# GpSimd issues the old rows of a batch, then the new rows of the batch before it

## The reference, cut to what matters

```python
x = x + einsum('bct,bcd->bdt', x, w0[cond])              # layer 0
q, k, v = x @ Wq.T, x @ Wk.T, x @ Wv.T                   # layer 1: 8 query heads, 4 key heads of 64
q, k = rope(rms(q)), rope(rms(k))
k_blocks = k_blocks.at[blk, :, off, :].set(k)            # all batches write their new rows first
v_blocks = v_blocks.at[blk, :, off, :].set(v)
k_all, v_all = k_blocks[block_tables], v_blocks[block_tables]
scores = q . k_all * SCALE, masked to the last 256 positions
x = x + softmax(scores) . v_all @ Wo.T
x = x + x @ W2[id] + b2[id]                              # layer 2: a 512x512 matrix per batch
x = x + x @ W3.T + adapter(x)                            # layer 3
```

## Time and profile before

| | |
|---|---|
| three runs | 1181.35, 1186.06, 1185.53 us (median 1185.53) |
| profiled execution | 1187.99 us, of which its span 1186.2 us |
| mean granted TensorE clock | 0.955 of full |
| PE busy | 1058.9 us (89% of the span) |
| DVE, ACT busy | 653.4 us (55%), 539.3 us (45%) |
| POOL busy | 532.8 us (45%) |
| gathers of old rows, L971 | 192, 999 ns each; POOL idle ahead of them 132.8 us |
| gathers of new rows, L981 | 192, 990 ns each; POOL idle ahead of them 281.7 us |

### The profile page before, as it was taken

The page is one execution under the profiler, slowest core; times in us unless marked ns, Lnnn a source line. Parts: engine busy times, 40 slices in busy tenths (PEclk is TensorE's granted clock), DMA queues, the critical chain, the costliest instruction groups (busy, mean ns, idle before and its releaser), DMA issues.

```text
span 1186.2 us, 23800 instructions
## 1 busy us (share of the span) xinstructions
PE 1058.9 (89%) x6440; PEld 709.0 (60%) x6440; DVE 653.4 (55%) x1888; ACT 539.3 (45%) x1336; POOL 532.8 (45%) x597
## 2 busy tenths in 40 slices
PE   4999999999159799999999999999999999999997
PEld 2767777877135556556556656556656556656555
DVE  5889785377234455555555555545555545455542
ACT  3457765475134344434444434444444444444440
POOL 1545444245545545544545444545544544444400
PEclk9999998899657899999999999999999999999998
DMA  3334443353263566655666655666655666655640
GB/s 123 115 134 142 136 138 110 109 175 134 82 203 98 159 203 211 191 178 172 196 193 205 203 180 172 195 192 212 198 180 172 193 192 206 203 181 173 196 143 18
DMA packets 95336, 196.15 MB, mean 165 GB/s; under 512 B 31346, under 2 KB 40114, under 8 KB 87110
## 3 DMA queue, kind: packets, MB, share of 16 engines
q1 hardware_dynamic: 63942, 149.49, 37.5%
q0 software_dynamic: 30784, 44.16, 14.2%
q10 hardware_dynamic: 576, 2.10, 0.5%
HBM read 195.08 MB, written 33.56 MB: 193 GB/s over the span
## 4 chain that ended last, share of the span: by engine, by line
PE 55%; DVE 5%; issue 3%; ACT 3%; DMA 1%; ACTq 0%; DVEq 0%
PE bank L90 18%; PE bank L1292 10%; PE bank L1246 8%; PE bank L1267 8%; PE bank L1233 4%; PE bank L1254 4%; DVE SM L1130 3%; ACT PT L1052 2%; PE bank L1223 2%; ACT KT L1052 1%; DVE XAL L1124 1%; DVE XAM L1173 1%; DMA KV<-kv_scratch,idxs 1%; DVE XAH L1178 1%; DVE nb L1134 0%
## 5 line engine op out<-in xcount | busy, mean ns | idle before, releaser
L981 POOL DMA_INDIRECT KV<-kv_scratch,idxs x192 | 190.1, 990 | 281.7 <-DMA KV<-in_pool,idxs 242.7
L1130 DVE CUSTOM_DVE_ANT_0 SM<-bank,FM 128x336 f32<-128x336 f32 x256 | 129.8, 507 | 249.7 <-PE bank L1246 228.7
L971 POOL DMA_INDIRECT KV<-in_pool,idxs x192 | 191.8, 999 | 132.8 <-issue 75.8
L1052 ACT ACTIVATE PT<-bank 112x384 f32<-112x384 f32 x256 | 111.7, 487 | 291.8 <-PE bank L1254 291.0
L1061 ACT ACTIVATE PR<-SM,nb 128x336 f32<-128x336 f32 x256 | 146.0, 577 | 1.0 <-DVE nb L1134 0.8
L1267 PE MATMUL bank<-PT,KV 112*64 112x128 f32 x1536 | 114.0, 285 | 27.4 <-ACT PT L1052 27.4
L1267 PEld LDWEIGHTS bank<-PT,KV 112*64 112x64 f32 x1536 | 86.6, 139 | 77.1 <-issue 40.0
L1052 ACT ACTIVATE KT<-bank 128x336 f32<-128x336 f32 x128 | 57.7, 451 | 159.7 <-PE bank L1233 159.1
L1292 PE MATMUL bank<-W,XT 128*64 128x512 f32 x512 | 123.7, 604 | 0.7 <-ACT XT L1052 0.7
L1246 PE MATMUL bank<-KT,QB 64*128 64x336 f32 x512 | 112.0, 515 | 5.6 <-ACT KT L1052 5.1
L90 PE MATMUL bank<-wqh,XTH 128*128 128x512 f32 x256 | 108.3, 423 | 9.2 <-DVE XTL L480 8.7
(11 more groups left out here) (157 smaller groups left out, 1931.5 us busy)
## 6 DMA issues: line engine op xcount, KB each, us to landing
W<-in_w SPq DMA_DIRECT2D x64, 1024.0 KB, 8.4
FM<-mask SPq DMA_DIRECT2D x64, 168.0 KB, 4.1
X<-in_x SPq DMA_DIRECT2D x32, 256.0 KB, 2.9
x_scratch<-X SPq DMA_DIRECT2D x32, 256.0 KB, 2.1
kv_scratch<-KVR SPq DMA_DIRECT2D x32, 256.0 KB, 2.4
qt_scratch<-QT SPq DMA_DIRECT2D x32, 256.0 KB, 2.9
QB<-qt_scratch SPq DMA_DIRECT2D x32, 256.0 KB, 2.8
XB<-x_scratch SPq DMA_DIRECT2D x32, 256.0 KB
```

Of the source, the lines that this page charges most:

```text
L971: pool.indirect_dma_start(out=KV[k][:, c, :], out_offset=None, in_=t["pool"], in_offset=bass.IndirectOffsetOnAxis(ap=idxs[k][:, c:c + 1], ...
L981: pool.indirect_dma_start(out=KV[k][:, c, :], out_offset=None, in_=kv_d, in_offset=bass.IndirectOffsetOnAxis(ap=idxs[k][:, NCH + c:NCH + c ...
L1052: return nc.scalar.activation(dst, src, ACT.Copy)
L1130: v.tensor_tensor_reduce(out=SM[u % 2][:, :], in0=bank[u % 2][:, 0:SPAN], in1=FM[k][:, :], scale=1.0, scalar=-3e38, op0=ALU.add, op1=ALU.m ...
```

## The change

In `body` on GpSimd the two helpers are called in another order, and `fresh` is moved out of `body` and takes the pair as an argument. Each batch's new rows are now issued one step later, behind the old rows of the batch that follows it. The last batch's new rows are issued behind the loop.

```diff
-                    def fresh(b):
-                        k = 2 * pr.par + b
...
-                    for b in range(2):
-                        held(b)
-                        fresh(b)
+                    held(0)
+                    if not (isinstance(p, int) and p == 0):
+                        fresh(pr.move(-1), 1)
+                    held(1)
+                    fresh(pr, 0)
+
+                def fresh(pr, b):
+                    k = 2 * pr.par + b
+
+                    wait_all(pool, s_pass_pool, (s_old[k], at(pr.i, 16 * NCH, 16 * NCH - 1)))
+                    for c in range(NCH):
+                        pool.indirect_dma_start(
...
                 bodies(pool, body)
+                fresh(Pair(PAIRS // 2 - 1, 1), 1)
```

More of the change, by code:

```diff
@@ L974, in held @@
                                 bounds_check=NPOOL * BLOCK - 1, oob_is_err=False).then_inc(s_old[k], 16)
-                    def fresh(b):
-                        k = 2 * pr.par + b
[L979 to L984, removed]
-                    for b in range(2):
-                        held(b)
-                        fresh(b)
+                    held(0)
[8 more added lines that the diff above has]
+                        pool.indirect_dma_start(
+                            out=KV[k][:, c, :], out_offset=None, in_=kv_d,
+                            in_offset=bass.IndirectOffsetOnAxis(ap=idxs[k][:, NCH + c:NCH + c + 1], axis=0),
+                            bounds_check=NB * T - 1, oob_is_err=False).then_inc(s_new[k], 16)
                 bodies(pool, body)
+                fresh(Pair(PAIRS // 2 - 1, 1), 1)
             @block.sync
```

## The result

The changed kernel takes 1370.12 us, median of 4 runs (1367.64 to 1371.04); the kernel before, in the same measurement, 1183.44 us (1180.84 to 1186.06). The ratio is 1.156, with a 95% interval of 1.150 to 1.162. The profiled execution of the changed kernel took 1369.77 us, its span is 1367.9 us and its mean granted clock 0.884, against 0.955 before. In the changed file the lines behind the change have moved: keys L1236, scores L1249, values L1270, expert products L1295, new-row gathers L987, expert matrices L1023.

What follows compares the result with a forecast made beforehand. The prediction took PE to set the pace. From the profiled 1188.0 us, + 86.8 standstill + 46.2 clock - 3.4 start of phase two = 1317.6, less 2.5 to the median of the runs: 1315 us, range 1215 to 1390.

Steps and rivals of the forecast that it cites:

- main story: Middle pairs: PE stands still about 3 us in each, clock halved behind some; 1265 to 1365 us, chance 0.60.
- the fourth rival: Middle pairs: landings at 8.2 us and the clock halved in every pair, 209.7 us more, 1392 us; chance 0.08.
- POOL's 242.7 us are worth nothing: POOL's waits for landed old rows, 242.7 us: removing them gains almost nothing behind 400 us, since PE sets the pace.
- The third gather meets the matrices: Batch 1's third new-row gather, middle pairs: issued 0.13 us behind the expert matrices, lands after 7.2 us, due within 4.1.
- 28 x 3.1: Pairs 3 to 30, PE waiting for batch 1's new rows: 3.1 us of standstill a pair, 86.8 us in all.
- The trace has one case of just this: Pair 2 before the change: new-row gathers issued around the expert matrices landed after 3.9, 7.2 and 8.2 us; PE stood 4.74.
- As if every second standstill halved the clock: Clock behind the standstills in 28 pairs: 1.65 us each, the middle of 0 to 3.3, 46.2 us in all.
- Start of phase two: First pairs: first product 1.8 us later but absorbed, batch 1's new rows 0.7 earlier, waits of 1.75 and 0.95 gone; 3.4 us won.
- Pair 2 pays as before: Pair 2: its 4.74 us wait for new rows stays, as its gathers still meet the expert matrices; no change in time.
- New rows of batch 0 are free: Middle pairs: batch 0's new rows land at 584.6 or 589.7 us, due about 593; at least 3 us of cover, no cost.
- the first (it works as its words say): Middle pairs: the third gather gets through ahead of the matrices; 1174 us, or 1182 if pair 2 alone stalls; chance 0.18.
- The second: Middle pairs: the gather waits for one matrix packet, lands after 5.75 us, standstill 1.65 us a pair, full clock; 1228 us, chance 0.14.

## Why the prediction was right, and where it was off

The prediction was 1315 us, in the range 1215 to 1390; the measured time is 1370.12. Its direction and its mechanism hold, two of its terms were too small. The main story's own range was 1265 to 1365, and the measured time lies 5 us above it; the wider range reached it because it went up to the fourth rival.

- **POOL's 242.7 us are worth nothing: right.** They went entirely and came back as waits for PE.
- **The third gather meets the matrices: right.** It was forecast 0.13 us behind them and due 4.1 us from its issue; in the pair shown it is 0.17 us behind and due 4.10 us from its issue. Over 29 pairs the offset is -0.28 to 0.83 us. The later the gather, the longer PE tends to stand still, with much scatter: 3.2 us on average in the 6 pairs with an offset up to 0.02, 3.4 in the 9 between 0.02 and 0.25 (1.6 to 5.1), 4.4 in the 11 between 0.25 and 0.5, 5.9 in the 3 above 0.5. The table above, 3.2 us to land away from the matrices and 6 to 8 beside or behind them, whether three or six stand in a row, shows the matrices as the cause of the late landing.
- **Size of the standstill: too small.** The term "28 x 3.1" measured 28 x 3.97, 24.4 us more. I had taken the middle one of the three landings of the earlier trace rows, 7.2 us; the third's own was 8.2, and 8.2 gives 4.15. The trace had the better value: the gather issued behind the matrices is the one to compare with. "The trace has one case of just this" was also too narrow: the new rows of batch 0 were issued 3.4 to 5.7 us behind the matrices in pairs 4 to 30 of before, and landed in 6.2 us. The earlier trace rows hide this; with records missing for the other buffers, its median of 3.1 us is that of the 48 gathers of batch 1 of the even pairs alone.
- **The clock: too small, and this is the largest error.** "As if every second standstill halved the clock" measured as every standstill, the 1.62 us one too: 28 x 2.88 in the place of 28 x 1.65, 34.4 us more. Between 0.8 us, which left the clock alone, and 4.74 us, which halved it, I had put the price in the middle. "Between the two nothing is known" overlooked a row at the end of the trace of before:

```profile
1174.74 0.33 PE L90 MATMUL bank<-XTH,wlh 128*128 128x128 f32 x1 [1.41 <-DVE XTL L1124]
```

  The clock is at 0.50 from 1175.09 to 1181.9 us there. Three waits of 0.7 to 0.9 us stand within 9 us ahead of this one, so it isn't a clean case, but it pointed to the full price. The size once the clock is halved was right: forecast 3.3 us, measured 2.88 on average.
- **Start of phase two: 6.0 us won, not 3.4, and for another reason.** The first product came 1.84 us later, as forecast (1.8), and the long wait fell by 2.75 us, nearly the 1.8 + 0.7 that the working implies. But neither of the two short waits went: 1.75 and 0.95 us became 0.88 and 2.02. The interval of pair 0 fell from 30.4 to 21.8 us, of which 3.6 are waits; the rest goes with the clock, which before stays at 0.50 until 373 us and after is at 1.00 from 336 to 346 us. No clock had been credited there, so that the term has the right sign and came this near is in part luck.
- **Pair 2 pays as before: right.** Its interval is 33.63 us, 33.40 before.
- **New rows of batch 0 are free: right in the result.** PE's 28 waits are one a pair, all at the keys of batch 1. In the experiments' measurements their lag costs 5% by itself; the waits there are for ScalarE, as in the late signals.

The terms close: 1188.0 + 111.3 + 80.7 - 6.0 - 3.0 (phase one) = 1371.0 us, against 1369.77 for the profiled execution. The 80.7 in this is a difference; the 81.6 us that PE is busy longer stand for it independently.

Of the rivals, the first (it works as its words say) fell with the 28 waits. The second had the gather wait for one packet of the matrices and land at 5.75 us: one pair of 29 is at or below that. So the price that this rival put on the rule of the Trainium skill, "DMA: Bandwidth & Descriptors", section "Queues, rings and completion order", by which engines go round their queues by whole packets, is too low here. The rule itself isn't tested: the rival took a whole matrix for one packet and let the gather wait once, and neither follows from the rule. What the trace shows is that GpSimd's queue moved 19 packets in 2.4 us, so it does get turns, and that the gathers still land 4.4 us later than without the matrices beside them. The fourth (1392 us) came nearest, at 4.15 and 3.34 us a pair against 3.97 and 2.88. Its reason, a longer gap ahead of the new rows, was not what happened: the gap is 0.30 us.

Open: why signals come late in the experiments' measurements. What the rows show is that ScalarE starts 4.4 us behind the product it waits for, while POOL issues six gathers in a row, and that it starts 1.4 to 1.8 us behind the end of the last. Part of the semaphore records is missing in these traces: of the 768 updates for the new rows of each buffer the repeat of the changed kernel has 321 to 377, the result's trace 761 to 768. So which signal is held up, and where, can't be read, and whether the recording itself has a part in it isn't known. Since pauses after three gathers brought nothing back, the row of gathers isn't shown as the cause either. Whether the changed kernel without the matrices beside its gathers would be as fast as the kernel before is open for the same reason.

## What to carry to other kernels

Before a wait is taken from an engine, look whether anyone waits for that engine: POOL's 242.7 us were slack, and what they held in place was the distance between the gathers and the 1 MB loads. When small transfers move in a program, write down what large ones are issued within a microsecond of them, and how long until they are due; price the delay by the landing of that transfer of the trace that stood on the same side of the large one. And count a standstill of PE, once it is longer than the short waits that the trace shows at full clock, with the clock behind it: here 3.97 us of waiting cost 6.85.

## What the hardware showed that I had not expected

- A standstill of PE of 1.62 us was followed by a granted clock of 0.50 over at least 6.6 us; in the kernel before, waits of up to 0.8 us (for ScalarE) in every pair were not.
- Three gathers issued 3.4 to 5.7 us behind two 1 MB loads still landed in 6.2 us (median), against 3.2 us away from them.
- In the measurements of the experiments, six gathers of GpSimd in a row (7.6 us from the first's start to the last's end) went with a ScalarE copy that started 4.4 us late, and PE stood still 2.9 to 3.1 us in each of 28 pairs; with nine in a row it was 7.2 us. In the result's measurement the same six gathers went with a copy on time. The kernel before differs little between the two (1183 us, and medians of 1206 to 1213 us, 2 to 2.5%), the changed kernel more (1370 and 1420 us, 4%).
